# Keys and queries of an attention layer turned through DRAM and VectorE, with the turn's work in a new order

## The reference

```
xn  = layernorm(x)
q   = rms_norm(xn @ q_w.T + q_b) * norm_q_w        # 16 heads of 32
k   = rms_norm(ctx @ k_img_w.T + k_img_b) * norm_k_img_w
v   = ctx @ v_img_w.T + v_img_b
x2  = x + tanh(g_xattn) * (softmax(q k.T / sqrt(32)) v @ o_w.T + o_b)
f   = layernorm(x2)
y   = relu(f @ up_w)**2 @ down_w + (f @ expert_weight) * (sum of the top 2 of f @ gate_w)
out = x2 + tanh(g_ffn) * (layernorm(y) * ln_gamma + ln_beta)
```

## Time and profile before

| | |
|---|---|
| time, median of 3 runs | 1360.54 us (1359.68 to 1361.13) |
| the profiled execution | 1360.45 us |
| its span, first to last instruction | 1358.7 us |
| TensorE busy | 1321.8 us |
| VectorE, ScalarE, GpSimd busy | 928.9, 615.9, 531.9 us |
| TensorE's mean granted clock | 0.995 |
| moved by DMA | 214.37 MB, mean 158 GB/s |

### The profile page before, as it was taken

One profiled execution on the slowest core, in us unless ns is written; L12 is line 12 of the kernel. 1 busy time (PEld: TensorE's weight loads), 2 busy tenths in 40 slices (PEclk: granted clock), 3 DMA queues, 4 the chain that ended last, 5 costly groups with the idle time before them and its releaser, 6 DMA issues.

```text
span 1358.7 us, 27965 instructions
## 1 busy us (share of the span) xinstructions
PE 1321.8 (97%) x9148; PEld 1127.2 (83%) x9148; DVE 928.9 (68%) x1768; ACT 615.9 (45%) x1891; POOL 531.9 (39%) x671
## 2 busy tenths in 40 slices
PE   6899999999999999999999999999999999999996
PEld 4688888888888888888888888888888888888984
DVE  5566666666666666886875775775785776776764
ACT  4788887778877777432312213213213123213110
POOL 3566666666666776451140140140240240230111
PEclk9999999999999999999999999999999999999998
DMA  6245555555544531539459358358468368377541
GB/s 234 70 126 149 147 144 139 149 154 156 146 129 129 141 87 64 188 123 254 138 150 253 130 156 255 125 158 255 135 169 247 122 176 245 111 182 220 178 143 33
DMA packets 279123, 214.37 MB, mean 158 GB/s; under 512 B 186640, under 2 KB 186768, under 8 KB 279056
## 3 DMA queue, kind: packets, MB, share of 16 engines
q1 hardware_dynamic: 246800, 154.78, 40.7%
q10 hardware_dynamic: 32256, 58.73, 13.0%
HBM read 163.92 MB, written 49.55 MB: 157 GB/s over the span
## 4 chain that ended last, share of the span: by engine, by line
PE 75%; issue 11%; DVE 6%; POOL 2%; ACT 1%; DMA 0%; ACTq 0%; DVEq 0%; POOLq 0%
PE bank L76 15%; PE bank L77 15%; PE bank L78 15%; PE wide L77 6%; PE wide L76 6%; PE wide L78 6%; PE bank L364 4%; PE wide L342 2%; PE wide L376 2%; PE bank L327 2%; DVE c L1341 1%; POOL yrstd L1833 1%; DVE yst L1712 1%; POOL yvar L1831 1%; ACT prob L683 0%
## 5 line engine op out<-in xcount | busy, mean ns | idle before, releaser
L1608 ACT ACTIVATE hT_hi<-c 128x512 fp32r<-128x512 f32 x128 | 80.0, 631 | 403.1 <-PE wide L78 220.1
L1840 POOL TENSOR_TENSOR pair<-pair,beta 128x512 f32<-128x512 f32 x28 | 39.3, 1405 | 453.3 <-DMA pair<-x_scratch 453.3
L683 ACT ACTIVATE prob<-wide,nmx 128x128 f32<-128x128 f32 x512 | 181.8, 401 | 64.9 <-DVE nmx L501 61.6
L77 PE MATMUL wide<-wo_lo,hT_hi 128*128 128x512 f32 x512 | 203.3, 397 | 0.0
L78 PE MATMUL wide<-wo_hi,hT_lo 128*128 128x512 f32 x512 | 201.9, 394 | 0.0
L76 PE MATMUL wide<-wo_hi,hT_hi 128*128 128x512 f32 x512 | 201.6, 394 | 0.0
L843 POOL TENSOR_TENSOR prob<-prob,rr 128x512 f32<-128x512 f32 x128 | 136.9, 1070 | 84.0 <-DVE rr L509 82.4
L1686 DVE TENSOR_TENSOR hT_lo<-c,hT_hi 128x512 fp32r<-128x512 f32 x128 | 97.0, 777 | 74.9 <-ACT hT_hi L1608 74.6
L683 ACT ACTIVATION_READ_ACCUMULATOR prob<-wide,nmx 128x1 f32 x512 | 123.6, 241 | 0.0
L78 PEld LDWEIGHTS wide<-wo_hi,hT_lo 128*128 128x128 f32 x512 | 96.1, 188 | 22.9
L76 PEld LDWEIGHTS wide<-wo_hi,hT_hi 128*128 128x128 f32 x512 | 96.2, 188 | 21.5
(11 more groups left out here) (229 smaller groups left out, 3564.2 us busy)
## 6 DMA issues: line engine op xcount, KB each, us to landing
wo_hi<-ring_scratch ACTq DMA_DIRECT2D x110, 256.0 KB, 3.7
wo_lo<-ring_scratch ACTq DMA_DIRECT2D x110, 256.0 KB, 4.5
wo_hi<-ring_scratch SPq DMA_DIRECT2D x46, 256.0 KB, 2.7
wo_lo<-ring_scratch SPq DMA_DIRECT2D x46, 256.0 KB, 3.0
fx<-x_scratch SPq DMA_DIRECT2D x36, 256.0 KB
xin<-in_x SPq DMA_DIRECT2D x32, 256.0 KB, 3.2
cin<-in_ctxT SPq DMA_DIRECT2D x32, 256.0 KB, 2.9
xres<-in_x SPq DMA_DIRECT2D x32, 256.0 KB, 4.0
```

The costliest lines, as they stand in the source:

```text
L77: eng.matmul(dst, ah, bl, start=False, stop=False)
L683: i = act.activation(prob[par][:, g, h * P:(h + 1) * P], cols(bank[g], h), ACT.Exp, bias=nmx[:, n:n + 1], scale=1.0, accum_out=rs[:, n:n + 1])
L1608: return act.activation(dst, src, ACT.Copy)
L1840: pool.tensor_tensor(res(g, j), res(g, j), ff.beta[:, :], ALU.add).then_inc(ff.po_r, 1)
```

## The change

For batches 3 to 30 keys and queries now go the way that x goes: SyncE stores kf and qf scattered (`deal`), loads them back (k_dealt, q_dealt), and VectorE turns their blocks into kT and qT. Their transposes on TensorE and the copies on ScalarE go. Batches 0 to 2 and 31 keep them. All block transposes, that of x too, now write their blocks in runs of 32; the columns then lie in another order, which is undone as the products read their moving operand: keys with a step of 32 elements (`by_key`), transposed probabilities with a step of 8 (`by_query`).

The turn is laid out anew on every engine. TensorE: keys projection, queries projection, all four transposes of the probabilities of a, scores(s), values(a), values projection of n, output projection of a, in the same turn (before: of o). The exponentials and the division of group 3 move to the start of the next turn. ScalarE's copies of pT stand ahead of the turn's exponentials. Psum banks are given out anew, turns -1 and 0 get an order of their own (`opening`), and the drain has one output projection less.

```diff
+            def deal(eng, src, there, s):
+                there = there.rearrange("(i b) (c k d) -> (b c) k i d", i=HG, c=KT, k=KT)
+                eng.dma_start(there, src[:, :].rearrange("p (k i d) -> p k i d", k=KT, i=HG)).then_inc(s, DMA)
+            def by_key(a):
+                return a.rearrange("p (c b) -> p b c", c=KT)
+            def by_query(b, a):
+                if isinstance(b, int) and b < XD - 1:
+                    return a
+                if is_slot(b, NB - 1):
+                    return a.rearrange("p (c b) -> p b c", c=KT)
+                return a.rearrange("p (h l) -> p l h", l=8)
...
# SyncE, slot
                     if has(a):
                         at_least(sp, dv_x2, a - 1, apart=True)
                         load(a, 1 - par, t["x"], xres, ld_r)
+                    if has(o):
+                        at_least(sp, dv_x2, o + 1, apart=True)
+                        sp.dma_start(x2_dram[o], x2[par][:, :]).then_inc(st_x2[par], DMA)
...
+                        deal(sp, xn, xd_dram[par], st_xd)
                     if has(s + 4):
                         load(s + 4, par, t["x"], xin, ld_x)
+                    if kq_dealt(n):
+                        at_least(sp, dv_kf, n + 1, apart=True)
+                        deal(sp, kf, kd_dram[1 - par], st_kd)
+                    if dealt(n + 1):
+                        at_least(sp, st_xd, dealt_count(n + 1), apart=True)
+                        at_least(sp, dv_xt, n + 1 - XD, apart=True)
                         sp.dma_start(x_dealt[:, :], xd_dram[par]).then_inc(ld_xd, DMA)
+                    if kq_dealt(n):
+                        at_least(sp, ac_qf, n + 1, apart=True)
+                        deal(sp, qf, qd_dram[1 - par], st_qd)
+                        at_least(sp, st_kd, dealt_count(n), apart=True)
+                        at_least(sp, dv_kT, n - XD, apart=True)
+                        sp.dma_start(k_dealt[:, :], kd_dram[1 - par]).then_inc(ld_kd, DMA)
                     if has(s + 4):
                         at_least(sp, ac_c, s + 3, apart=True)
                         at_least(sp, po_c, s + 3, apart=True)
                         load(s + 4, par, t["ctxT"], cin, ld_c)
                     if ff.has_half(s - 3):
                         ff.q_store(sp, s - 3, 1 - par)
                     if ff.has_half(s - 1):
                         ff.q_load(sp, s - 1, 1 - par)
+                    if kq_dealt(n):
+                        at_least(sp, st_qd, dealt_count(n), apart=True)
+                        at_least(sp, dv_qT, n - XD, apart=True)
+                        sp.dma_start(q_dealt[:, :], qd_dram[1 - par]).then_inc(ld_qd, DMA)
...
# TensorE, slot (new)
+                    at_least(pe, po_c, n + 1)
+                    at_least(pe, dv_aT, o + 1)
...
+                    mm3(pe, BK, cT[1 - par], wk).then_inc(pe_K, 1)
+                    at_least(pe, dv_xT, n + 1)
...
+                    mm3(pe, BQ, xT, wq).then_inc(pe_Q, 1)
+                    at_least(pe, dv_vb, s + 1)
+                    turn_probs(a, 1 - par, 0)
+                    at_least(pe, dv_kb, n + 1)
+                    turn_probs(a, 1 - par, 1)
+                    if has(o):
+                        at_least(pe, dv_x2, o + 1)
...
+                    turn_probs(a, 1 - par, 2)
+                    at_least(pe, dv_qb, n + 1)
+                    turn_probs(a, 1 - par, 3)
+                    scores(s)
+                    probs_taken(pe, a, 1)
+                    values(a, 1 - par)
...
+                    mm3(pe, BV, cT[1 - par], wv).then_inc(pe_V, 1)
...
+                    project_out(a, BO)
# TensorE, drain (new, its first part)
+                    scores(s)
+                    probs_taken(pe, a, 0)
+                    ff.turn(pe, 0, t_first)
+                    pe.wait_ge(dv_x2, o + 1)
+                    turn_probs(a, a % 2, 3)
+                    probs_taken(pe, a, 1)
+                    ff.turn(pe, 1, t_first)
+                    probs_taken(pe, a, 2)
+                    values(a, a % 2)
+                    project_out(a, BO)
+                    ff.turn(pe, 2, t_first)
...
# VectorE, slot (new)
+                    lo_xT(n)
+                    if has(o):
+                        residual_sum(o, par, BO)
+                        inverse(a, 3)
+                    if kq_dealt(s):
+                        turn_q(s)
+                    add_bk(n)
+                    if has(n + 1):
+                        normalise(n + 1, par)
+                    add_bq(n)
+                    scale_k(n)
+                    if has(s + 3):
+                        stats(s + 3, 1 - par)
...
+                    maxima(s, 0)
+                    maxima(s, 1)
+                    maxima(s, 2)
+                    split_values(a)
+                    maxima(s, 3)
+                    inverse(s, 0)
+                    bias_v(n, 1 - par)
+                    inverse(s, 1)
+                    if dealt(n + 1):
+                        turn_x(n + 1)
+                    inverse(s, 2)
+                    if kq_dealt(n):
+                        turn_k(n)
# ScalarE, slot (new)
+                    if has(o):
+                        exps(a, 1 - par, 3)
+                    square_k(n)
+                    if has(n + 1):
+                        hi_ctx(n + 1, par)
+                    if ff.has_half(s - 2):
+                        ff.q_split_hi(act, s - 2, par)
+                    take_probs(a, 0)
+                    square_q(n)
+                    take_probs(a, 1)
+                    take_probs(a, 2)
+                    take_probs(a, 3)
+                    scale_q(n)
+                    hi_aT(a)
+                    if not kq_dealt(n):
+                        take_kT(n)
                     exps(s, par, 0)
                     exps(s, par, 1)
+                    if not kq_dealt(n):
+                        take_qT(n)
                     exps(s, par, 2)
                     if has(n + 1):
                         hi_xT(n + 1)
```

More of the change, by code:

```diff
@@ L413, in slot @@
-                    if is_slot(n, 0):
-                        keep_clock(BV, 4, D)
-                    if has(n):
-                        at_least(pe, dv_kf, n + 1)
-                        if has(a):
-                            probs_taken(pe, a, 2)
-                        turn(kf, BTK, pe_Tk)
-                    if is_slot(n, 0):
-                        keep_clock(BV, 8, D)
-                    if has(a):
-                        for g in range(NG):
-                            values(a, 1 - par, g)
@@ L584, in slot @@
-                    if has(s):
-                        inverse(s, 3)
-                    if starting:
-                        stats(1, 1)
-                        at_least(dve, pe_Q, n + 1)
-                        dve.tensor_tensor(as_strips(qb[:, :]), as_strips(BQ), by_strip(bq[:, :]), ALU.add).then_inc(dv_qb, 1)
-                    if has(n + 1) and not has(a):
-                        normalise(n + 1, par)
+                        dve.wait_ge(ld_bk, DMA)
+                        add_bk(n)
@@ new lines, in opening, with slot @@
+                    for k in range(KT):
+                        weight_lo(3, k)
+                    dve.wait_ge(ld_bo, DMA)
+                    dve.wait_ge(s_tanh, 1)
+                    dve.tensor_scalar(tgbo[:, :], tgbo[:, :], tanh_g[:, 0:1], None, ALU.mult).then_inc(cst, 1)
+                def slot(s, par):
+                    if isinstance(s, int) and s < 1:
+                        return opening(s, par)
+                    a, n, o = s - 1, s + 1, s - 2
+                    lo_xT(n)
@@ L592, in slot @@
                     if has(o):
                         residual_sum(o, par, BO)
-                    if starting:
-                        for k in range(KT // 2, KT):
-                            weight_lo(2, k)
-                    if has(s + 3) and not starting:
-                        stats(s + 3, 1 - par)
-                    if has(a):
-                        split_values(a)
-                    if dealt(n + 1):
-                        turn_blocks(n + 1)
-                    if starting:
-                        stats(2, 0)
@@ new lines, in opening, with slot @@
+                    exps(s, par, 3)
+                    square_q(n)
[3 more added lines that the diff above has]
+                    take_qT(n)
+                    hi_xT(n + 1)
+                    for k in range(KT):
+                        weight_hi(3, k)
+                def slot(s, par):
+                    if isinstance(s, int) and s < 1:
+                        return opening(s, par)
+                    a, n, o = s - 1, s + 1, s - 2
```

469 lines of the change are left out of this document (245 added, 224 removed).

## The result

The changed kernel takes 1383.35 us (1383.1 to 1386.45, 4 runs), the kernel before 1360.11 (1359.22 to 1361.13, 4 runs) beside it: ratio 1.0176, 95% interval 1.0158 to 1.0194. That is slower by 23 us, where 1326 was forecast with a range up to 1360. It is rival 1 in its form "both by two", which had 1385 and a part of the 0.19 for slower.

The account below looks back on a forecast made before the run. TensorE, busy 1321.8 of 1358.7 us, was taken as the bound. Shorter turns (28 x 1.1 = 31 us) plus the ends gave 35.1, so 1360.45 - 35.1 = 1325.3, forecast 1326; range 1316 to 1360.

Parts of the forecast that it names:

- rival 1: Strided moving operands slow TensorE's scores and values: 1417 or 1385, values alone 1356; chance 0.19 slower, 0.08 small form.
- both by two: Scores and values on TensorE each take twice as long, (1.01 + 1.10) x 28 = 59 us: 1385.
- The strided operands: TensorE's scores read keys with step 32, values read pT with step 8; extra cost taken as 0.
- or its small products stretch: Sign that the prediction is wrong: TensorE's scores and values groups lengthen from 1.0 and 1.1 us, 3 or more.
- The bound above: Upper bound for strided values on TensorE: memory gives one value instead of four, 4 x 1.01 = 4.04 us.
- The turn apart from that: TensorE's new turn: 16.12 less 0.94 for two transposes and 0.15 for edges, 15.0 us; bounds 14.85 and 15.2.
- The queries' round trip: Scaled queries are stored scattered and loaded last on SP's queue, at about 13.8, landing 3.2 into the next turn; no stall.
- the bound of 1: Upper bound on the stall from the round trips, 1 us in each of the 20 loaded turns; 0 was taken.
- rival 2: The queries' round trip comes late in the 20 loaded turns, 0.5 to 1 us a turn: 1336 to 1346; chance 0.13.
- 0.4 of cover: Slack on VectorE behind the queries' load: queries' bias done at 6.45 plus waits, against 6.85; beyond it lateness costs one to one.
- The place that the prediction called tight: ScalarE's copy of probability transpose 1 stands behind the queries' square; copies end 8.85, fourth values group starts 9.1, cover 0.3.
- Both ends: Opening and drain: turns 2 to 29 start at 59.0, turn 30 takes 16.0, drain 16.8 (uncertain by 2); last transpose 511.8.

Follow-up runs that it names:

- the early load: SyncE issues the dealt queries' load straight behind the ctx load: 1337.13 us with operands read in a row, 1338.69 with block transposes writing every fourth element.
- the version in natural order: Changed kernel, but block transposes write every fourth element, no product reads with a step, and the dealt queries' load goes straight behind the ctx load: 1338.69 us.
- the kernel with step 1: Changed kernel, but scores and values read keys and probabilities as they lie, so heads see them in mixed order: 1358.0 us, ratio 0.9959 to the kernel before.

## Why the prediction was wrong, point by point

**The step that failed: "The strided operands", "I take 0, since a single stream has the slack of two".** The term measured 0.88 a turn for scores and 0.97 for values, 1.85 together; over 27 turns 50 us. It is also the sign that the prediction named for being wrong: "or its small products stretch". The argument was that fp32 reads its columns at half the pace of fp32r (0.86 against 0.44 ns) and so has a factor of two in hand. The runs with steps show how much of that is so: fp32 bears step 2, which fp32r does not, and neither bears step 4. That fits a slack which covers a step of 8 bytes; the change used 32 and 128. (The two kinds of product differ in more than their type, four strips at once against the whole array, and that wasn't taken apart.) The bound above, four times, was twice too high: four column strips that read at once lose a factor of 1.96 (values), four row strips 1.80 (scores). The Trainium skill's rule (Advanced Engine Details and Errata, section Memory Cachelines: a 16-byte line should be hit at least twice) put the threshold where the fp32 runs put it: free with two hits, dear with one. The prediction named it, saw that both patterns break it, and let an argument outweigh it that rested on no row with a step. In fp32r its "at least twice" wasn't enough: step 2 has two hits a line and cost double. That rival 1's 1385 lies so near 1383.35 is in part luck: it added 59 for steps to 1326, where the steps cost some 53 and the kernel without their price and with the early load came to 1337 or 1339.

**The turn apart from that: right.** Turn 2 and both kernels with the early load run at 15.05 (forecast 15.0), as the sum of a smaller 0.87 and a larger 0.2, two errors that cancel.

**The queries' round trip: the forecast "I take no stall" was wrong too, though the changed kernel hides it.** Without the steps 18 loaded turns came to 16.14 each, 1.09 over 15.05 and just beyond the bound of 1; by itself that is rival 2 at its far end. The issue position was right (in the changed kernel 274.54, that is 14.05 into its turn; forecast 13.8), and a landing 4.2 us after the issue is near the 4.4 of the earlier trace rows. Mis-sized was what lies behind: I charged lateness one to one against 0.4 of cover, but kf's store closes a loop of waits, and a late VectorE meets GpSimd: kf took 1.75 in place of the 0.75 of before and waited 0.86 for rk (below). From kf's start the round went 8.6 us to the load's issue (276.17 to 284.73), where I had 7.05 to 13.8, 6.75. That the cover depends on one place in SyncE's queue is shown by the moved issue: VectorE's waits for the queries fell from 39.6 to 2.7 us (step 1, 100 to 400 us) and the time by 21.

**VectorE: right within 0.6 us a turn.** 11.7 of 15.0, that is 78%, was forecast for writes in runs of 32; 74% with these and 80% with every fourth element were measured (100 to 400 us, early load); the block transposes took 0.69 and 1.09 (forecast 0.69, 1.08).

**ScalarE, GpSimd, DMA share: right.** With step 1 and the early load ScalarE is busy 78%, GpSimd 67% and the DMA engines 0.88 (100 to 400 us), where 79, 71 and 0.88 were laid out. The place that the prediction called tight, ScalarE's copies ahead of the last values group, gave way only while VectorE was late (0.59).

**Both ends: too good by 3 us.** In the version in natural order turn 2 starts at 59.68 against 59.0, turn 30 lasts 15.9 against 16.0, and the drain 19.2 against 16.8: from 503.55 to the last feed-forward transposes at 522.77. Its waits on TensorE:

```profile
506.36 1.17 PE L392 MATMUL wide<-kT,qT 32*128 32x128 f32 x32 [1.24 <-ACT prob L783]
...
508.98 0.63 PE L404 MATMUL bank<-ident,prob 128*128 128x128 f32 x4 [0.85 <-POOL prob L956]
...
512.78 0.50 PE L76 MATMUL bank<-wo_hi,aT_hi 128*128 128x512 f32 x1 [1.73 <-DVE aT_lo L534]
```

The one on aT_lo was forecast as 2.1, and two later ones as 0.7 and 0.5 (0.34 and 0.33); the scores' wait of 1.24, for exponentials that the new order puts into the next turn, and the 0.85 for their division were not. No kernel was run on the drain by itself. The range's low end, 1316, comes to 1318.5 by its own terms (28 turns at 14.85, drain without its 3.3 of waits).

**What is left between 1326 and 1338.7.** The last feed-forward transposes come at 522.77, 11.0 after the forecast's 511.8: opening 0.7, 28 turns at 15.05 in place of 15.0 1.5, turn 30 and drain 2.3, and 6.4 in late turns: from scores to scores, four of them between 353.05 and 449.77 last 0.33, 2.2, 3.53 and 0.35 longer than 15.05. In the two dear ones TensorE waits 1.39 and 2.93 before Q for the lo part of x. VectorE, which makes it, has waited 1.07 for x and 2.06 for the keys' load in the first of them, and 3.85 for x in the second:

```profile
426.11 1.08 DVE L574 STREAM_TRANSPOSE x_turned<-x_dealt 128x512 f32<-128x512 f32 x1 [3.85 <-DMA x_dealt<-xd_scratch]
```

In the second SyncE's issue of the xin load, ahead of kf's store, took 4.65 us (414.46 to 419.11), in turns in which the first feed-forward loads join the traffic and the DMA share from 420 to 440 us is 0.87. With step 1 the late turns cost 2.5. That SyncE's long issue is the cause is read from this one trace; whether another order on its queue takes these 2 to 6 us back wasn't tried. Two more microseconds lie behind these transposes: they come 24.2 earlier than before, the span is only 22.2 shorter. No run shows why.

**The changed kernel's own sum.** Its last feed-forward transposes come at 569.10, 57.3 after the forecast's: opening 0.4, 28 turns 51.6 (27 x 1.86 and 28 x 0.05), turn 30 1.7 (its scores and values have steps), drain 3.6, of which 2.4 are there in the version without steps too and 1.2 came with the steps of the last two batches' values. Less the 35.1 that was forecast, 22.2 us later than before, which is the difference of the spans, 1381.0 and 1358.7.

## What to carry to other kernels

Before an operand of a matrix product is read with a step, count how many of its elements lie in 16 bytes: in these runs the fp32 products paid nearly double below two, the fp32r ones double below four, and no more for larger steps (up to 32 elements in fp32, 4 in fp32r); let the writer do the reordering where the writer has time. When a stage is full on one engine, lay out the round trips as loops too, from the store that a late consumer delays to the load that it waits for, and put that load ahead of traffic that is not needed so soon. And take each half of a change by itself: here the dearer products hid a loop of waits, and one fix without the other moved the time by 2% or nothing.

## What the runs showed of the hardware

The price of a step in the moving operand, as time from start to start:

| product | step 1 | step 2 | step 4 | step 8 | step 32 |
|---|---|---|---|---|---|
| a batch's scores (16 products, 32 in the rows), fp32, 128 columns, 4 row strips | 1.10 | 1.12 | 2.01 | | 1.98 |
| its values (the same), fp32, 128 columns, 4 column strips | 1.01 | 1.04 | 1.94 | 1.98 | |
| one of 512 columns, fp32r | 0.23 | 0.46 | 0.46 | | |

VectorE's kf instruction (one scalar and two tensor operands) took 0.75 in the kernel before. Its group there, and in the kernel with step 1 (100 to 400 us; busy, mean ns):

```profile
L582 DVE SCALAR_TENSOR_TENSOR kf<-kb,rk,nqk 128x512 f32<-128x512 f32 x19 | 14.3, 752 | 22.6 <-POOL rk L821 22.6
```

```profile
L556 DVE SCALAR_TENSOR_TENSOR kf<-kb,rk,nqk 128x512 f32<-128x512 f32 x19 | 33.3, 1752 | 14.0 <-POOL rk L937 13.9
```

In the kernel with step 1 GpSimd starts its lo part of the context 0.06 ahead of it:

```profile
276.11 1.27 POOL L946 TENSOR_TENSOR eight<-cin,eight 128x512 fp32r<-128x512 f32 x1
```

GpSimd ends at 277.38, kf at 277.92, 0.54 later. In the changed kernel GpSimd's instruction runs from 265.93 to 267.21 and kf from 266.74 to 267.75, again 0.54 after GpSimd's end, and in the version in natural order 277.21 and 277.76, 0.55. So kf did not run slower beside GpSimd; by these ends it stood until GpSimd was through. The Trainium skill, SBUF — State Buffer, section SBUF: two separate sides, says that a VectorE instruction with two inputs in SBUF and a GpSimd instruction that reads SBUF lock each other out for a whole instruction; the trace agrees, with 0.54 to 0.55 in three kernels. In the kernel with step 1 kf so lost 1 us in each of 19 turns (1.75 against 0.75), inside the loop of waits. How much of the longer turn is due to it was not tested by itself.
